# Adding the two halves of each exponential tile on VectorE before the denominator matmul, in an eight-core attention and FFN layer

## What is computed

```python
q = _rms_norm(q)
k = _rms_norm(k)
k = jnp.repeat(k, rep, axis=1)
v = jnp.repeat(v, rep, axis=1)
attn = jnp.einsum('bhqd,bhkd->bhqk', q, k) * scale
attn = jax.nn.softmax(attn, axis=-1)
y = jnp.einsum('bhqk,bhkd->bhqd', attn, v)
vn = v / jnp.maximum(jnp.linalg.norm(v, axis=-1, keepdims=True), L2_EPS)
y = y - jnp.sum(y * vn, axis=-1, keepdims=True) * vn
```

## Time and profile before

| | us |
|---|---|
| median of five runs | 4864.01 |
| lowest and highest of them | 4819.33, 5146.47 |
| the profiled execution, its time | 4826.45 |
| the profiled execution, span of the slowest core (core 0) | 4824.8 |
| spans of the other seven cores | 4799.3 to 4824.7 |
| attention stage, first scores to last reciprocal | 1160.8 to 3009.5 |

### The profile page before, as it was taken

The page is one execution under the profiler, slowest core; times in us unless marked ns, Lnnn a source line. Parts: engine busy times, 40 slices in busy tenths (PEclk is TensorE's granted clock), DMA queues, the critical chain, the costliest instruction groups (busy, mean ns, idle before and its releaser), DMA issues.

```text
span 4824.8 us, 45795 instructions; the slowest of 8 cores (4799.3 to 4824.8 us)
## 1 busy us (share of the span) xinstructions
PE 3582.8 (74%) x15606; PEld 1315.0 (27%) x15606; DVE 1164.4 (24%) x2188; ACT 1423.9 (30%) x1714; POOL 96.0 (2%) x155
## 2 busy tenths in 40 slices
PE   2455577778888899999999888144358888888991
PEld 0222233333222222222222222022123333333340
DVE  0332577774111111111111111133220000000004
ACT  0111233333555555555555555011000000000001
POOL 0000000000000000000000000000000000000010
PEclk9767799999998999999999998566679999999995
DMA  8000422220000000000000000611322233223444
GB/s 140 18 27 18 145 92 96 97 97 31 3 3 3 3 3 3 3 3 3 3 3 3 3 3 1 152 57 52 45 44 53 53 57 57 53 53 54 67 69 147
DMA packets 74671, 218.61 MB, mean 45 GB/s; under 512 B 16232, under 2 KB 42344, under 8 KB 61120
## 3 DMA queue, kind: packets, MB, share of 16 engines
q0 software_dynamic: 55632, 91.95, 11.9%
q1 hardware_dynamic: 18816, 123.74, 7.5%
HBM read 279.26 MB, written 28.31 MB: 64 GB/s over the span
## 4 chain that ended last, share of the span: by engine, by line
PE 70%; DVE 15%; DMA 4%; ACT 4%; issue 3%; another core or an unknown queue 3%; DVEq 0%; POOL 0%; ACTq 0%; SPq 0%; POOLq 0%
PE S_ps L167 12%; PE dn_ps L167 11%; PE yT_ps L167 10%; PE gps L167 7%; PE ups L167 7%; PE ops L167 6%; PE kps L167 4%; PE vps L167 4%; PE wops L167 3%; PE qps L167 3%; DVE rdn_sb L167 2%; DVE st L167 2%; DVE xnT L167 1%; DVE khat L167 1%
## 5 line engine op out<-in xcount | busy, mean ns | idle before, releaser
L167 ACT ACTIVATE P_sb<-S_ps 128x1024 bf16<-128x1024 f32 x1024 | 1048.6, 1024 | 805.3 <-PE S_ps L167 774.9
L167 PE MATMUL S_ps<-qth,KT_sb 128*128 128x512 bf16 x2048 | 655.3, 407 | 17.3 <-ACT P_sb L167 13.5
L167 PE MATMUL yT_ps<-P_sb,V_sb 128*128 128x512 bf16 x2048 | 624.4, 387 | 0.0
L167 PE MATMUL dn_ps<-P_sb,onec_sb 128*1 128x512 bf16 x2048 | 609.6, 379 | 0.0
L167 DVE RECIPROCAL rdn_sb<-dn_ps 1x512 f32<-1x512 f32 x32 | 107.1, 3346 | 1446.4 <-PE dn_ps L167 1446.4
L167 PE MATMUL kps<-wk_sb,xnT 128*128 128x512 bf16 x1024 | 407.1, 398 | 0.4
L167 PE MATMUL vps<-wv_sb,xnT 128*128 128x512 bf16 x1024 | 405.5, 396 | 0.0
L167 PE MATMUL gps<-xn2T,wg_sb 128*128 128x512 bf16 x1376 | 323.1, 389 | 13.3 <-DMA wu_sb<-wu_r 12.6
L167 PE MATMUL ops<-wdq_sb,hid 128*128 128x512 bf16 x1376 | 313.4, 388 | 19.0 <-DMA wdq_sb<-wd 11.2
L167 PE MATMUL ups<-xn2T,wu_sb 128*128 128x512 bf16 x1376 | 311.0, 379 | 0.0
L167 ACT ACTIVATE sg_sb<-gps 128x512 bf16<-128x512 f32 x86 | 51.4, 597 | 770.7 <-PE ups L167 770.7
(11 more groups left out here) (144 smaller groups left out, 2093.8 us busy)
## 6 DMA issues: line engine op xcount, KB each, us to landing
xa<-x_my SPq DMA_DIRECT2D x72, 1024.0 KB, 4.8
wg_sb<-wg_r POOLq DMA_DIRECT2D x43, 512.0 KB, 5.1
wu_sb<-wu_r POOLq DMA_DIRECT2D x43, 512.0 KB, 7.1
wdq_sb<-wd POOLq DMA_DIRECT2D x40, 512.0 KB, 5.5
wq_sb<-wqT POOLq DMA_DIRECT2D x1, 8192.0 KB, 79.4
wo_sb<-woT POOLq DMA_DIRECT2D x4, 2048.0 KB, 45.8
out<-x_sb SPq DMA_DIRECT2D x8, 1024.0 KB, 4.8
x2r_sb<-out SPq DMA_DIRECT2D x8, 1024.0 KB, 6.8
```

What stands on the lines that cost most here:

```text
L167: instr = getattr(eng, op)(*a, **kw)
```

## The change

In each group, VectorE adds the two halves of `P_sb` into one of two new buffers `padd`, 128x512 bf16. TensorE then multiplies the column of ones by `padd` in one matmul, where it had one for each half. The addition is recorded one step of the loop before the denominator matmul that reads it, and at the head of the loop body. It waits for the exponential of its group and for the denominator matmul of two groups ago, which read the same buffer. ScalarE, before it writes `P_sb` anew, now also waits for the addition of four groups ago.

```diff
+    padd = [bC.enter_context(nc.sbuf_tensor(f"padd{i}", [128, 512], BF16)) for i in range(2)]
...
+            paddd = {}
+            dnd = {}
             for gi in range(NG + 2):
+                if 1 <= gi <= NG:
+                    g = gi - 1
+
+                    @on("vector")
+                    def _(v, g=g):
+                        dve.wait(v)
+                        act.wait(v, e_done[g])
+                        pe.wait(v, dnd.get(g - 2, 0))
+                        dve.inc(v.tensor_tensor(padd[g % 2][:, :], P_sb[g % 4][:, 0:512],
+                                                P_sb[g % 4][:, 512:1024], ALU.add))
+                    paddd[g] = dve.n
...
                         if g >= 4:
                             pe.wait(a, pv_done[g - 4])
+                            dve.wait(a, paddd[g - 4])
                         act.inc(a.activation(P_sb[g % 4][:, :], S_ps[gp][:, :], AF.Exp))
...
-                        for j in range(2):
-                            pe.inc(te.matmul(
-                                dn_ps[:, :], onec_sb[:, :], P_sb[g % 4][:, j * 512:(j + 1) * 512],
-                                start=(g == 0 and j == 0), stop=(g == NG - 1 and j == 1)))
+                        dve.wait(te, paddd[g])
+                        pe.inc(te.matmul(
+                            dn_ps[:, :], onec_sb[:, :], padd[g % 2][:, :],
+                            start=(g == 0), stop=(g == NG - 1)))
                     pv_done[g] = pe.n
+                    dnd[g] = pe.n
```

## The result

| | before | changed | ratio, 95% interval |
|---|---|---|---|
| lowest of all runs, us | 4819.33 | 4709.69 | |
| median of all runs, us | 4849.19 | 4788.19 | |
| profiled execution, us | 4826.45 | 4718.08 | |
| ratio, see below | | | 0.976 [0.9712, 0.9808] |

The kernel became 2.4% faster; the prediction was 4707 us on the footing of the profiled execution, where the ratio gives 0.976 × 4826 = 4710 us. In some executions of every kernel here the cores of one die show a lower clock: the medians of all runs contain them, the ratios leave them out, and where such an execution was the profiled one, a core of the other die is read.

A forecast was written before the change was run, and what follows sets the result against it. TensorE was taken to set the attention loop's pace. Per block 58.01 − 6.67 (removed matmuls) + 1.64 (late addition) + 1.4 (clock) = 54.4 us; 119 us saved in all, 4826.45 to 4707 us, range 4650 to 4770.

The forecast's parts named there:

- The bound and the removed matmul: Steady group: TensorE sets the period; one denominator matmul less takes 0.215 us off, 1.49 to 1.28 us.
- The addition: VectorE, each group: one bf16 addition 128x512 takes 0.42 us, hidden in steady state with over 1 us of cover.
- The wait on TensorE: Steady group, ahead of the denominator's weights: the new wait costs 0, upper end 0.05 us per group.
- exposed wait: Rival, steady group: the new wait ahead of the denominator's weight load costs 0.051 us each, about 4757 us; chance 0.12.
- The late first addition: Block head: first addition queues behind VectorE's correction, so group 3's scores come 1.64 us later, in 31 blocks.
- The clock: Block head: TensorE's hole of 1.8 us keeps or brings the clock low, costing 1.4 us, bounds 0 and 2.0.
- clock is kept: Rival, block head: the hole doesn't lower the clock, the 1.4 us aren't paid, 4664 us; chance 0.20.
- the one sign of being wrong that came true: Behind the hole at a block's head: wrong if the low clock there lasts over 4 us.
- The 10.7 us at which the change would have lost: Rival "the clock does not come back", behind the hole: break-even at 10.7 us of 1.2 GHz; about 4880 us at 15; chance 0.06.
- ScalarE: the step that failed: Steady group: exponentials back to back take 1.17 us, 1.19 with one more wait, so ScalarE stays hidden under TensorE's 1.28.
- period falls to ScalarE's 1.19: Rival, steady group: a single denominator matmul lets one gap go, 1.28 becomes 1.19 us, 4626 us; chance 0.06.

The follow-up runs named there:

- the later runs: Changed kernel with one denominator matmul for every second group, VectorE adding two groups' tiles: ratio 0.9789; the same with ScalarE waiting for its scores alone: ratio 0.9446.
- the filled hole: Changed kernel plus five matmuls of unused result on TensorE ahead of the wait for a block's first addition: 4664.48 us, ratio 0.9724.
- two waits: Changed kernel without ScalarE's waits on the matmuls and on the addition of four groups ago: 4711.40 us, ratio 0.9775.

## Why the prediction was right, point by point

- **The bound and the removed matmul.** TensorE's stream set the period and each removed matmul gave 0.215 us: 1.49 to 1.28. Right, and with ScalarE's two waits removed, when it could go at 1.17, the period was still TensorE's 1.28.
- **The addition.** 425 ns, forecast 400 to 420 from the slope between the 1-column and 128-column rows. Right. The slope itself is a little steeper than worked out, 0.52 ns per column: the 1024-column addition of the later runs took 693 ns where 640 would follow from it.
- **The wait on TensorE.** Nothing exposed in the steady group. Right, and the rival "exposed wait" is out.
- **The late first addition.** Forecast 6.0 us behind the scores, measured 6.15 to 6.5, 6.21 on average. The step from the correction to the addition took 0.24, not 0.13: an operation behind three waits takes longer to start than the rows with one wait. Right in mechanism, 0.2 short in size. The hole is 1.9 to 2.6 us long, forecast 1.8.
- **The clock.** Forecast 1.4 us a block, 1.46 net by the filled hole, 1.72 in the loop alone. That the low clock returns or stays behind the hole was seen in 29 of 31 blocks; the rival "clock is kept" happened in the other two. Each us of low clock cost 1.72/3.84 = 0.45 us, forecast 0.47. How long it lasts was put at some 3 us, and it is 3.84 on average and over 4 in eleven blocks: this is the one sign of being wrong that came true, and it is worth 0.3 us a block. The 10.7 us at which the change would have lost are far off.
- **ScalarE: the step that failed.** "Plus one more semaphore wait of 17 ns: 1.19, under 1.28." The row with 1.17 is of a block's first groups, which by the code have two waits; from the fifth group on the changed kernel has four. So two more waits were to be added, not one, and each costs 0.05 to 0.06 us, not 17 ns; the trace of before shows 1.23 behind three. The real floor with four waits is 1.28, a dead heat with TensorE. It went unpunished in the steady group only because the two numbers are equal, which is luck, and it shows at the block's tail. ScalarE lags, so the last denominator matmul started 1203.61 − 1200.64 = 2.97 us behind the last scores, not 2.63. The rival "period falls to ScalarE's 1.19" was no rival at all: with half the denominator matmuls it had its chance and the period stayed.
- **What was left out.** The clock falls later behind the reciprocal in many blocks (4.4 us behind it in the second, where before had 1.8), so the broadcast runs partly at full clock: the median broadcast matmul took 814 ns against 1056 before. Two of them make a broadcast, so some 0.4 us a block come back.

Where a block's time lies, in us, mean of the 31 blocks behind the first on the core shown above; the forecast's parts are worked out from its terms:

| | before | forecast | changed | hole filled | two waits |
|---|---|---|---|---|---|
| reciprocal to first scores | 7.69 | 7.69 | 7.26 | 7.50 | 6.91 |
| first scores to first denominator matmul | 4.12 | 6.03 | 6.21 | 6.21 | 6.14 |
| from there to the last score matmul | 42.63 | 37.74 | 38.00 | 36.28 | 38.57 |
| last score matmul to reciprocal | 3.57 | 2.92 | 3.20 | 3.22 | 2.97 |
| the block | 58.01 | 54.38 | 54.67 | 53.21 | 54.59 |
| low clock behind the first denominator matmul | 0.23 | 3 | 3.84 | 0 | 5.19 |

The forecast is 0.3 us short as a whole: 0.2 by the late addition, 0.3 by the clock and 0.3 by ScalarE's lag at the tail, less the 0.4 that the broadcast gave back. That it came so near is in part luck: three terms that were too small and one that was left out nearly cancelled. Without its clock term the forecast has 37.74 − 1.4 = 36.34 for the loop, and the filled hole, which has no low clock there, took 36.28.

The reading of the broadcast rests on these rows of the changed kernel and of before (ns: shortest, median, longest):

```profile
L167 PE MATMUL bc_ps<-rdn_sb,onerf_sb x64: 587/814/1188, 1207.6 to 2903.3; 1*128 1x512 f32 x64
```

```profile
L167 PE MATMUL bc_ps<-rdn_sb,onerf_sb x64: 587/1056/1188, 1214.5 to 3013.9; 1*128 1x512 f32 x64
```

and on the clock of the changed kernel behind its second reciprocal:

```profile
1259.10:1263.40 4.30, 0.81 (x2) 0.29 (x2) 3.34 (x1) 0.00 (x0) 0.00 (x0) 1.00 0.00 0
1263.50:1270.20 6.70, 4.42 (x13) 1.30 (x12) 4.34 (x15) 2.76 (x3) 0.00 (x0) 0.50 0.13 39
```

## What to carry to other kernels

When work moves to an idle engine, look at what stands in that engine's queue at the edges of the loop, not at its average load: here sixteen small operations in front of the first addition took back over a quarter of what the removed matmuls gave, and the hole they made cost nearly as much again in clock. Before counting an engine as spare, work out its floor with all of its waits in a row from a stretch where it runs back to back under those very waits, and drop those waits that another wait already covers. If an engine's work is halved and the period doesn't move, the other engine's floor has been found.

## What the runs showed of the hardware

- Exponentials of 128x1024 start 1.28 us apart at best behind four waits, 1.23 behind three, 1.17 behind two, and 0.92 or less behind one that isn't on ScalarE itself; each lasts 1.02 us by its row, so without the wait on their own engine they overlap.
- With a hole of 1.9 to 2.6 us in TensorE's work some 4 us after a block's first scores, the clock behind it was at 1.2 GHz for 3.84 us of dense work on average (not at all in 2 of 31 blocks, over 4 us in 11); with the hole filled by useless matmuls it was at 2.4 GHz in all of them, and a block took 1.46 us less. With nineteen useless matmuls in the epilogue it stayed at 2.4 GHz, one stretch of 3.4 us apart. By the Trainium skill (TensorE: Matmul & The Clock Gate, "Why this matters for your kernels") the clock is lost only to idle gaps between bursts that are longer than these; here 1.9 us of idle before the change were enough, and in the changed kernel a hole of 2.17 us with busy stretches on both sides, and the measurement decides.
- Going from weights of 128 columns to one of a single column and back leaves a gap of 0.10 us each time at 2.4 GHz, whether two matmuls stand between (0.52 to the next start) or one (0.31).
- Addition in bf16 from SBUF: 425 ns for 512 columns and 693 for 1024, 0.52 ns per column.
